# Cross-attention of a perceiver block: one of three key transposes and its eviction placed between the keys and the values of a chunk

## The reference

```python
q = _ln((x @ Wq + bq).reshape(b, s1, H, HD), qn_w, qn_b)          # H = 16 heads of HD = 32
kv = jnp.concatenate([y_main @ Wk + bk, y_main @ Wv + bv], axis=-1)
k = _ln(kv[..., :HD], kn_w, kn_b)
v = kv[..., HD:]
ctx = _attn(qT, k.transpose(0, 2, 1, 3), v.transpose(0, 2, 1, 3))      # softmax(q k / sqrt(32)) v
ctx_dca = _attn(qT, k_dca.transpose(0, 2, 1, 3), v_dca.transpose(0, 2, 1, 3))
return (ctx + ctx_dca) @ Wo + bo
```

## Time and profile before

| | |
|---|---|
| median of 3 runs | 1621.39 us (1620.69 to 1623.71) |
| the profiled execution | 1622.73 us, of which its span is 1620.9 us |
| PE busy | 1539.4 us, 95% of the span |
| DVE, ACT, POOL busy | 52%, 46%, 29% |
| mean granted clock of PE | 0.980 |

### The profile page before, as it was taken

One profiled execution on the slowest core, in us unless ns is written; L12 is line 12 of the kernel. 1 busy time (PEld: TensorE's weight loads), 2 busy tenths in 40 slices (PEclk: granted clock), 3 DMA queues, 4 the chain that ended last, 5 costly groups with the idle time before them and its releaser, 6 DMA issues. The chain is left out here.

```text
span 1620.9 us, 41874 instructions
## 1 busy us (share of the span) xinstructions
PE 1539.4 (95%) x16226; PEld 1301.7 (80%) x16226; DVE 847.4 (52%) x1793; ACT 740.6 (46%) x1515; POOL 464.6 (29%) x492
## 2 busy tenths in 40 slices
PE   5789999999999999999999999999987998899999
PEld 2378888888888888888888888888865666899998
DVE  6755555555655555555564555555525554433333
ACT  2245555555555555555555555555532322311111
POOL 3233333333333333333333333333331000022102
PEclk9989999999999999999999999999988999699999
DMA  6021011000110100011000110100020000111011
GB/s 232 17 93 32 15 29 32 17 26 27 32 28 15 32 27 28 16 30 28 27 19 27 28 32 15 28 27 16 3 60 1 0 0 1 60 59 59 20 39 52
DMA packets 35920, 53.81 MB, mean 33 GB/s; under 512 B 7091, under 2 KB 15670, under 8 KB 35766
## 3 DMA queue, kind: packets, MB, share of 16 engines
q1 hardware_dynamic: 35332, 51.44, 10.4%
q10 hardware_dynamic: 434, 0.08, 0.0%
HBM read 48.89 MB, written 2.62 MB: 32 GB/s over the span
## 5 line engine op out<-in xcount | busy, mean ns | idle before, releaser
L1042 POOL TENSOR_TENSOR ksq<-kc 128x512 f32<-128x512 f32 x200 | 208.4, 1042 | 445.3 <-DVE kc L1087 443.4
L1087 DVE TENSOR_TENSOR kc<-psum,bk_sb 128x512 f32<-128x512 f32 x200 | 138.2, 691 | 235.1 <-PE psum L100 235.1
L954 ACT COPY v_sb<-psum 128x512 f32<-128x512 f32 x192 | 112.6, 587 | 292.8 <-PE psum L100 292.8
L968 ACT ACTIVATE probs<-psum 128x1024 f32<-128x1024 f32 x208 | 202.9, 1023 | 89.3 <-PE psum L1209 88.9
L1209 PE MATMUL psum<-qbd,k 64*128 64x128 f32 x3328 | 217.4, 280 | 4.2 <-issue 4.1
L1209 PEld LDWEIGHTS psum<-qbd,k 64*128 64x128 f32 x3328 | 196.2, 188 | 11.2 <-issue 6.9
L1035 POOL TENSOR_TENSOR y_lo<-y_sb,y_hi 128x256 fp32r<-128x256 f32 x190 | 139.6, 735 | 226.6 <-ACT y_hi L927 225.7
L1226 PEld LDWEIGHTS psum<-v_sb,probs 128*64 128x64 f32 x6144 | 187.3, 138 | 17.6 <-issue 17.5
L1226 PE MATMUL psum<-v_sb,probs 128*64 128x33 f32 x6144 | 198.0, 224 | 0.0
L1093 DVE TENSOR_REDUCE kss<-ksq 128x16 f32<-128x512 f32 x200 | 136.5, 682 | 111.4 <-POOL ksq L1042 111.4
L100 PE MATMUL psum<-wk_hi,y_hi 128*128 128x512 f32 x400 | 176.8, 442 | 10.8 <-issue 8.7
(11 more groups left out here) (223 smaller groups left out, 2310.9 us busy)
## 6 DMA issues: line engine op xcount, KB each, us to landing
y_sb<-in_y SPq DMA_DIRECT2D x48, 512.0 KB, 3.8
expert_raw<-in_wg SPq DMA_DIRECT2D x5, 768.0 KB, 4.6
expert_raw<-in_wu SPq DMA_DIRECT2D x5, 768.0 KB, 4.6
expert_raw<-in_wd SPq DMA_DIRECT2D x5, 768.0 KB, 4.5
out_dram<-x_sb SPq DMA_DIRECT2D x8, 256.0 KB, 2.0
x_sb<-in_x SPq DMA_DIRECT2D x1, 1536.0 KB, 10.4
wq<-in_wq SPq DMA_DIRECT2D x4, 256.0 KB, 4.7
xa_wo<-in_wo SPq DMA_DIRECT2D x1, 1024.0 KB, 12.2
```

What stands on the lines that cost most here:

```text
L968: nc.scalar.activation(probs[:, buf(u), :], psum[:, bank:bank + 2, :].rearrange("p a n -> p (a n)"), ACT.Exp, scale=SCALE).then_inc(s["ex" ...
L1042: nc.gpsimd.tensor_tensor(sq[:, buf(n)], kc[:, buf(n)], kc[:, buf(n)], ALU.mult).then_inc(s["ksq"], 1)
L1087: nc.vector.tensor_tensor(kc[:, buf(n)], psum[:, K_BANK, :], g.bk[:], ALU.add).then_inc(s["kb"], 1)
```

## The change

In a step that has more sets to turn than chunks to project, and at least one chunk to project, the first set is taken out of its place and put between K and V of the step's first chunk; the other sets move up by one. ACT evicts it before the values of that chunk. The condition holds in step 4 of each of the 8 passes and nowhere else.

```diff
@@ scalar engine, steps
                         project, turned, high = (projections(group + n, room) for n in (2, 1, 3))
+                        if len(turned) > len(project) > 0:
+                            k_evac(i, turned.pop(0))
                         for j in range(3):
                             if j < len(project):
                                 v_evac(i, project[j])
@@ matrix engine, steps
-                        for j in range(3):
+                        early = [turned.pop(0)] if len(turned) > len(project) > 0 else []
+                        for j in range(max(len(project), len(turned))):
                             if j < len(project):
                                 keys(i, project[j])
+                                for n in early:
+                                    turn(i, n)
+                                early = []
                                 if j == 0 and group in (0, 6):
                                     pe.wait_ge(s["oe"], i * 2 + (group // 6 + 1))
                                 values(i, project[j])
```

## The result

The changed kernel took 1611.36 us (median of 6 runs, 1610.10 to 1613.59) against 1621.29 us for the kernel before: a ratio of 0.9939, with a 95% interval of 0.9928 to 0.9950. The profiled execution has a span of 1611.1 us, 9.8 less than before.

What follows compares the result with a forecast made beforehand. PE's stream was taken to bound the kernel. Eight steps gaining 1.21 us each make 9.7 us, from the profiled 1622.73 to 1613.0, or 1611.7 allowing for that execution's 1.3 us above the median; range 1609.8 to 1614.6.

Steps and rivals of the forecast that it cites:

- What bounds it, and the hole: Cross-attention: PE's stream sets the end; a 1.26 us hole ahead of transposes 12 in step 4 of eight passes.
- Who ends the wait: Transposes 12 in step 4 wait for ACT's eviction of chunk 11 from one bank, 0.15 us hand-off, not DVE's keys.
- The sum for the step: Step 4 on PE, from K13 to the weighting: 7.04 us instead of 8.25, a gain of 1.21 us.
- The time: Whole kernel: eight steps gain 9.7 us, giving 1611.7 us; chance 0.82.
- The price of one more interruption: Step 4's projections: the first matmul after the additional transposes, V13, pays some 0.08 us more.
- The bound of 10.1 us: Eight steps 4: gain if the interruption cost nothing, 1.26 us a step, giving 1611.3 us.
- The estimate from the Trainium skill: Transposes inside step 4's projections: 0.32 us for four, nothing after them, 0.22 us less a step, time near 1610.
- The covers: Step 4 slack before moved work would wait: 0.21 us for T11, 1.6 for T12, 0.9 for seed 14.
- The second: Step 4: the hole moves to T11 because keys 10 are evicted late; 1612.5 to 1616.5 us, chance 0.07.
- The third: Steps after step 4: something else paces them and takes the gain back; 1621.4 us, chance 0.03.
- The fourth: Step 4: T12 waits for DVE's keys of chunk 13, losing 0.43 us a step; 1624.8 us, chance 0.05.
- the fifth: Step 4: transposes inside the projections make the chip grant a lower clock; 1668 us at half rate, chance 0.03.

Runs made afterwards that it cites:

- experiment 4: Kernel before, no order moved; the tail's transposes go into the keys' PSUM bank, idle at that moment: 1611.50 us, 0.9940 of before.
- experiment 2: Kernel before with only ACT's part of the change, the new order of evictions, PE left as it was: 1626.31 us, 1.0026 of before.
- experiment 3: Kernel before with DVE taking the head sums of 14 ahead of the scaling of keys 13: 1622.43 us, 0.9999 of before.
- experiment 6: Changed kernel with five otherwise unused copies on ACT ahead of the eviction of keys 10: 1621.88 us, 0.9993 of before.
- experiment 1: Changed kernel with ACT's evictions put back in the old order, leaving PE's part alone: 1641.45 us, 1.0121 of before.
- experiment 7: Changed kernel with the weighting of the step's last unit held back between second and third scores: 1609.70 us, 0.9919 of before.

## Why the prediction was right, step by step

- **What bounds it, and the hole.** Right. The eight holes of 1.0 us are gone from PE's waits, and their removal is the measured gain, with the change (9.35 us in the trace) as without moving anything (experiment 4).
- **Who ends the wait.** Right, against the name in the row. That chunk 13's scaling has nothing to do with it is shown by the changed kernel itself, in which T12 starts 1.62 us before it ends, and by experiments 2 and 3; that the bank is the cause by experiment 4, and the hand-off of 0.15 us came out as 0.14 and 0.15 in experiments 6 and 1.
- **The sum for the step.** 7.04 us forecast, 7.06 measured, term by term: K13 1.51, T10 0.35, V13 1.48, T11 0.35, K14 1.48, V14 1.36, T12 0.53. A pass, forecast to be 1.2 us shorter, is 1.17 shorter; K15 and V15 take 2.88 us together instead of 2.86, which the forecast put at nothing and no run explains.
- **The time.** 1611.7 us forecast, 1611.36 measured. That it fits to 0.3 us is in part luck: eight steps give 9.35 us in the trace, 9.7 were forecast, and the medians differ by 9.9, while the six runs of the changed kernel spread over 3.5 us.
- **The price of one more interruption.** I had charged some 0.08 us, and taken 1.26 us as the hole. Both were too high by the same 0.08 us or so, which cancels in the difference: a set costs 0.43 us inside the projections and beside another set alike (experiment 4). The bound of 10.1 us at the lower end of the range therefore stood on a hole that isn't there. The estimate from the Trainium skill (TensorE: Matmul & The Clock Gate, section Back-to-back issue gap), 0.32 us for four transposes, is not borne out: the trace has 0.35 to the next start here too, and the dearer first matmul behind it (V13 1.48 us against 1.36 for V14).
- **The covers.** T11's was forecast at 0.21 and is 0.26, since the eviction starts 0.64 us after T10 and not 0.68. That it had to be there, and that ACT's part of the change is what makes it, is shown by experiments 1 and 6. The seed of 14 was forecast to end at 158.54, or 158.62 with the 0.08 us by which this profile's step begins later; it ends at 158.64.
- **The rivals.** The second didn't happen but can be made to (experiment 6). The third, a gain taken back later, didn't either: the last pass still shows 9.35 us of it. The fourth is refuted. For the fifth, the clock of the step stayed at 1.00, with T10 and T11 both inside the projections.

The spans differ by 9.8 us, 0.5 more than the last pass's weighting moved (9.27). This rest lies behind that step, where the executions differ without any change of the order: by 1.3 us in the last scores (last section), and by up to 2.2 us from there to the end (425.1 to 427.3 us in the profiles of before, the change and experiments 3 and 4). So the rest is no effect that the runs tell from chance.

## What to carry to other kernels

Where two short pieces of work share one PSUM bank, the second pays for the whole eviction of the first; put other work of at least that length between them, or give one of them a bank that is idle at that moment. Moving the producer is half of it: the eviction must move to the same place in the evicting engine's queue, or the wait comes back larger than it was. A row's releaser can be an event that only happened to end in the same moment, as here in all eight passes: look up in the code what the wait asks for, find a second place with the same wait where the named engine is idle, and compare the hand-off times.

## What the runs showed of the hardware

The granted clock differs between executions in the same piece of the program. In the last scores of the cross-attention, behind the hole of the earlier trace rows, the stretch of the kernel before reads

```profile
1188.00:1196.00 8.00, 7.99 (x142) 7.47 (x142) 0.00 (x0) 3.46 (x4) 0.00 (x0) 0.79 0.01 2
```

a clock of 0.79, and the same stretch of experiment 3, which has the same order on PE and the same holes,

```profile
1188.00:1196.00 8.00, 7.47 (x178) 7.01 (x178) 0.00 (x0) 3.85 (x5) 0.00 (x0) 1.00 0.01 2
```

a clock of 1.00. Ahead of it the clock was 1.00 in both. From transposes 24 to the last weighting it took 7.27 us before (1187.99 to 1195.26) and 5.97 in experiment 3 (1188.25 to 1194.22), the same 5.97 as in the changed kernel (1178.74 to 1184.71), whose clock there was 1.00 too. So these 1.3 us are no effect of the change. Experiments 6 and 7 show the slower form in the same place (7.32 us from transposes 24 to the last weighting in experiment 7, at a clock of 0.77), and experiment 1 shows such a loss in its sixth pass, at a clock of 0.79, behind a hole of the same size (1.45 us). In each of these the drop came behind a hole of 1.3 to 1.5 us ahead of transposes, but most holes of that size had none behind them. What sets it in one execution and not in the other stays open.
